# A cross-attention pass of a decoder kernel: folded weights made one pass earlier, zero rows written by SyncE, and another order of the parts

## The reference, cut to what matters

```python
def _L1_xattn_ref(hidden_states, external_embeddings, Wq, bq, Wk, bk, Wv, bv):
    q = hidden_states @ Wq + bq
    k_tok = hidden_states @ Wk + bk
    v_tok = hidden_states @ Wv + bv
    k_ext = external_embeddings @ Wk + bk
    v_ext = external_embeddings @ Wv + bv
    s_self = jnp.einsum('bsh,bsh->bs', q, k_tok)[..., None]
    s_ext = jnp.einsum('bsh,beh->bse', q, k_ext)
    probs = jax.nn.softmax(jnp.concatenate([s_self, s_ext], axis=-1), axis=-1)
    return probs[..., :1] * v_tok + jnp.einsum('bse,beh->bsh', probs[..., 1:], v_ext)

x = x + _L1_attn_ref(_layernorm(x), ...)              # 16 heads of 16
x = x + _L1_xattn_ref(_layernorm(x), ctx_1024, ...)   # the pass that is changed
x = x + _L1_ffn_ref(_layernorm(x), ...)               # top 2 of 8 experts, weighted by their scores
```

## Time and profile before

| | |
|---|---|
| time, three runs | 2931.3, 2927.97, 2929.44 us (median 2929.44) |
| the profiled execution | 2933.47 us, span 2931.6 us |
| mean granted TensorE clock | 0.919 of full |
| TensorE busy | 2398.4 us (82%) |
| VectorE busy | 1984.3 us (68%) |
| ScalarE busy | 1442.5 us (49%) |
| GpSimd busy | 1361.2 us (46%) |
| 16 scatters of zeros twice, L1827 | 973 ns each |

### The profile page before, as it was taken

One profiled execution on the slowest core, in us unless ns is written; L12 is line 12 of the kernel. 1 busy time (PEld: TensorE's weight loads), 2 busy tenths in 40 slices (PEclk: granted clock), 3 DMA queues, 4 the chain that ended last, 5 costly groups with the idle time before them and its releaser, 6 DMA issues. The chain is left out here.

```text
span 2931.6 us, 49210 instructions
## 1 busy us (share of the span) xinstructions
PE 2398.4 (82%) x16164; PEld 1880.4 (64%) x16164; DVE 1984.3 (68%) x4760; ACT 1442.5 (49%) x2778; POOL 1361.2 (46%) x1281
## 2 busy tenths in 40 slices
PE   5888888399999479999999999868888775399880
PEld 3666666389999346566556566547777664399870
DVE  4888888466555268888878888726777665377783
ACT  3666666255555257777777777633333231222220
POOL 5777777454342354444444444114555555000475
PEclk9999999699999789999999999779999897699995
DMA  2222221332220001001001010022222222544795
GB/s 67 62 69 72 59 73 48 75 127 92 61 86 26 29 19 34 26 30 33 26 30 34 26 30 26 19 97 76 90 91 90 91 86 71 164 140 138 222 299 159
DMA packets 205352, 226.68 MB, mean 77 GB/s; under 512 B 32511, under 2 KB 190209, under 8 KB 204849
## 3 DMA queue, kind: packets, MB, share of 16 engines
q1 hardware_dynamic: 181712, 170.85, 18.8%
q0 software_dynamic: 22016, 50.58, 5.5%
q10 hardware_dynamic: 1376, 2.10, 0.2%
HBM read 131.99 MB, written 95.49 MB: 78 GB/s over the span
## 5 line engine op out<-in xcount | busy, mean ns | idle before, releaser
L1320 POOL TENSOR_TENSOR f_hm<-f_hm,f_mhalf 128x64 f32<-128x64 f32 x32 | 347.4, 10855 | 2.7
L1488 DVE TENSOR_REDUCE f_nm<-f_raw 128x4 f32<-128x1024 f32 x256 | 311.9, 1218 | 33.6 <-PE f_raw L1588 33.5
L1381 ACT ACTIVATE f_PT<-f_sco 128x1024 f32<-128x1024 f32 x256 | 262.6, 1026 | 84.6 <-PE f_sco L1606 81.4
L2325 POOL DMA_INDIRECT d_pick<-expert_out,e_out_slots x128 | 131.4, 1027 | 286.2 <-DMA expert_out<-d_eo 233.0
L1588 PE MATMUL f_raw<-f_k4T,f_q4T 64*128 64x256 f32 x1024 | 142.1, 359 | 37.7 <-DVE f_nm L1488 36.9
L895 ACT ACTIVATE b_hT<-b_H,b_b1r 128x512 f32<-128x512 f32 x128 | 88.4, 690 | 163.0 <-PE b_H L1024 147.8
L2344 ACT ACTIVATE d_hh<-d_H 128x512 fp32r<-128x512 f32 x78 | 46.6, 598 | 244.8 <-PE d_H L2438 244.8
L1588 PEld LDWEIGHTS f_raw<-f_k4T,f_q4T 64*128 64x128 f32 x1024 | 85.9, 207 | 106.0 <-DVE f_nm L1488 54.2
L1818 POOL DMA_INDIRECT expert_in<-g_xm,e_slots x128 | 128.6, 1005 | 39.6 <-issue 36.9
L1039 PE MATMUL b_O<-b_w2l,b_hTh 128*128 128x256 f32 x512 | 144.9, 283 | 0.0
L1039 PE MATMUL b_O<-b_w2h,b_hTl 128*128 128x256 f32 x512 | 144.7, 283 | 0.0
(11 more groups left out here) (364 smaller groups left out, 7868.2 us busy)
## 6 DMA issues: line engine op xcount, KB each, us to landing
d_xs<-expert_in SPq DMA_DIRECT2D x78, 256.0 KB, 3.1
expert_out<-d_eo SPq DMA_DIRECT2D x78, 256.0 KB, 2.2
x_scratch<-a_x SPq DMA_DIRECT2D x64, 256.0 KB, 2.7
b_w<-in_L_ffn_W_dram SPq DMA_DIRECT2D x16, 1024.0 KB, 5.7
a_x<-in_x_dram SPq DMA_DIRECT2D x32, 256.0 KB, 3.7
a_cx<-in_ctx_dram SPq DMA_DIRECT2D x32, 256.0 KB, 3.1
f_x<-x_scratch SPq DMA_DIRECT2D x32, 256.0 KB, 2.7
f_xr<-x_scratch SPq DMA_DIRECT2D x32, 256.0 KB, 2.7
```

Source lines behind the costliest of these rows:

```text
L1320: g.tensor_tensor(hm[b % 2][:, :], hm[b % 2][:, :], mhalf[:, :], ALU.pow).then_inc(hroot, 1)
L1381: s.activation(PT[n % 3][:, t, :, :], heads(SCO), ACT.Exp, scale=float(DH) ** -0.5).then_inc(probs_ready, 1)
L1488: v.tensor_reduce(nm[:, t, g * HG:(g + 1) * HG], heads(RAW), AX.X, ALU.max, negate=True)\
L2325: g.indirect_dma_start(pick[b % GR][:, t, c, :], None, ex.eo_d[k], bass.IndirectOffsetOnAxis(ap=ex.out_slots[:, b, t, c:c + 1], axis=0), b ...
```

## The change

Four edits. The fold moves into the first slot of `attention_pass`, behind the v product of batch 0, with banks X and Y for G0 and G1; Wq and Wk become two more weights of `Layer1Weights`, loaded in the phase before. The zero rows at the end of each expert's rows are written by SyncE: per block it reads eight row numbers into a register, each with a DMA of 256 rows. The parts of a slot get another order. Constants and tables that this makes idle go.

```diff
 class Layer1Weights:
+        self.wq_in = [sb("wq_in0", [P, C, D]), sb("wq_in1", [P, C, D])]
+        self.wqk, self.g0, self.wr, self.r0 = sb("wqk", [P, C, D]), sb("g0", [P, C]), sb("wr", [P, C]), sb("r0", [P, 1])
-        self.count = 12
+        self.count = 14
...
+        for tile, name in zip(self.wq_in, ("Wq", "Wk")):
+            weight(tile[:, :, :], by_chunk(a[f"L1_xattn_{name}"]))
...
 attention_pass, scalar, take_v:
+                if b == 0:
+                    fold_cross_weights()
+
+            def fold_cross_weights():
+                act.wait_ge(pro_psum, 1)
+                s.activation(wq_T[0][:, :, :], halves(X), ACT.Copy).then_inc(pro_sb, 1)
+                s.activation(wq_T[1][:, :, :], halves(Y), ACT.Copy).then_inc(pro_sb, 1)
+                act.wait_ge(pro_psum, 2)
+                s.activation(w.wqk[:, :, :], halves(X), ACT.Copy).then_inc(pro_sb, 1)
+                s.activation(w.g0[:, :], Y[:, 0:C], ACT.Copy).then_inc(pro_sb, 1)
...
 attention_pass, tensor, project_v:
+                if b == 0:
+                    fold_cross_weights()
+
+            def fold_cross_weights():
+                transposes(X, w.wq_in[0])
+                transposes(Y, w.wq_in[1]).then_inc(pro_psum, 1)
+                pe.wait_ge(pro_sb, 2)
+                wqT, wkT = wq_T
+                for m in range(C):
...
 cross_pass:
-        ORDER = ("sco gx", "gate norm", "pre stats", "sco scores", "gate T", "file rows", "pre norm", "mix mix", "pre cxT",
-                 "sco exp", "pre T", "mix T", "gate logits", "sco expT", "mix cross", "pre g", "gate ranks")
+        ORDER = (
+            "sco gx", "pre stats", "pre cxT", "gate norm", "sco scores", "gate T", "file rows", "pre norm",
+            "mix mix", "sco exp", "pre T", "sco expT", "mix T", "gate logits", "mix cross", "pre g", "gate ranks")
...
 cross_pass, sync:
-            for tile, name in zip(wq_in, ("Wq", "Wk")):
-                sync.dma_start(tile[:, :, :], by_chunk(a[f"L1_xattn_{name}"])).then_inc(w_in, 16)
...
+            def pad(k):
+                sync.wait_ge(pads_ready, k + 1)
+                for e in range(NE):
+                    row = sync.value_load(pad_row[k][0:1, e:e + 1], min_val=0, max_val=ex.xs_d.shape[0] - ex.TILE)
+                    sync.dma_start(ex.xs_d[bass.ds(row, ex.TILE), :].rearrange("(n p) d -> p n d", p=P),
+                                   zero[:, :].unsqueeze(1).broadcast_to([P, T, D])).then_inc(pads_filed, 16)
+
             for n in range(B + 2):
                 if n + 2 < B:
                     load_x4(n + 2)
                     load_cx(n + 2)
                 if n >= 2:
                     store(n - 2)
+                if n >= 5 and ex.block_of(n - 5)[1]:
+                    pad(ex.block_of(n - 5)[0])
+            pad(NB_ - 1)
...
+            sync.wait_ge(pads_filed, 16 * NE * NB_)
...
 cross_pass, gpsimd, file_rows:
-                k, last = ex.block_of(b)
-                if last:
-                    pool.wait_ge(pads_ready, k + 1)
-                    stand_alone(pool, pool_passed)
-                    for n in range(2):
-                        for e in range(NE):
-                            g.indirect_dma_start(ex.xs_d, bass.IndirectOffsetOnAxis(ap=zidx[k][:, n, e:e + 1], axis=0),
-                                                 zero[:, :], None, bounds_check=ex.xs_d.shape[0] - 1,
-                                                 oob_is_err=False).then_inc(pads_filed, 16)
...
 cross_pass, scalar and tensor: the fold and the waits for pro_sb go (the same instructions as above, with G0 and G1)
 cross_pass, vector:
-            dve.wait_ge(pro_sb, 6)
...
-                v.tensor_tensor(zidx[k][:, :, :], zrow[:, :].unsqueeze(2).broadcast_to([P, 2, NE]),
-                                carried[:, :].unsqueeze(1).broadcast_to([P, 2, NE]), ALU.add).then_inc(pads_ready, 1)
+                v.tensor_scalar(pad_row[k][:, :], carried[:, :], 1.0, None, ALU.add).then_inc(pads_ready, 1)
```

More of the change, by code:

```diff
@@ L1173, in attention_pass @@
         mhalf = sb("mhalf", [P, T * 2 * H])
+        wq_T = sbn("wq_T", 2, [P, C, D])
         selh = sb("selh", [P, H, DH])
@@ L1203, in attention_pass @@
         oT_ready, o_inv = sem("oT_ready"), sem("o_inv")
+        pro_psum, pro_sb = sem("pro_psum"), sem("pro_sb")
         rows = lambda t: t.rearrange("(b t p) d -> b p t d", t=T, p=P)
@@ L1548, in _ @@
             pe.wait_ge(w_centred, 3)
+            pe.wait_ge(w.loaded, 16 * w.count)
             def normT(b):
@@ L1566, in project_v @@
                 project(Z, xnT, wqkv[:, :, 2 * D:3 * D]).then_inc(full("in v"), 1)
+                if b == 0:
[6 more added lines that the diff above has]
+                for m in range(C):
+                    cols = slice(m * P, (m + 1) * P)
+                    for c in range(C):
+                        t_.matmul(halves(X)[:, m, :], wqT[:, c, cols], wkT[:, c, :], start=c == 0, stop=c == C - 1)
+                    for c in range(C):
+                        t_.matmul(Y[:, m:m + 1], wkT[:, c, cols], w.bqT[:, c:c + 1], start=c == 0, stop=c == C - 1)
+                    for c in range(C):
+                        t_.matmul(Y[:, C + m:C + m + 1], wqT[:, c, cols], w.bkT[:, c:c + 1], start=c == 0, stop=c == C - 1)
+                for c in range(C):
+                    last = t_.matmul(Y[:, 2 * C:2 * C + 1], w.bqT[:, c:c + 1].broadcast_to([P, P]), w.bkT[:, c:c + 1],
+                                     start=c == 0, stop=c == C - 1)
+                last.then_inc(pro_psum, 1)
             def splitT(r, b):
@@ L1614, in weigh @@
                 if g == 0:
+                    if b == 0:
+                        pe.wait_ge(pro_sb, 6)
                     wait_taken(pe, "in v", b)
@@ L1668, in cross_pass @@
         iota8 = sb("iota8", [P, NE])
[L1669 to L1672, removed]
+        wvx, bvx, gw, gb = w.wvx, w.bvx, w.gw, w.gb
+        wqk, g0, wr, r0 = w.wqk, w.g0, w.wr, w.r0
         XR, CR, YR = 4, 4, 3
@@ L1729, in slots @@
                         parts[part](b)
-        CONSTS = 14 + NB_
+        CONSTS = 13 + NB_
         block = ctx.enter_context(nc.Block())
@@ L2103, in _ @@
             pe.wait_ge(consts, CONSTS)
[L2104 to L2109, removed]
-                cols = slice(m * P, (m + 1) * P)
-                for c in range(C):
-                    t_.matmul(halves(G0)[:, m, :], wqT[:, c, cols], wkT[:, c, :], start=c == 0, stop=c == C - 1)
-                for c in range(C):
-                    t_.matmul(G1[:, m:m + 1], wkT[:, c, cols], bqT[:, c:c + 1], start=c == 0, stop=c == C - 1)
-                for c in range(C):
-                    t_.matmul(G1[:, C + m:C + m + 1], wqT[:, c, cols], bkT[:, c:c + 1], start=c == 0, stop=c == C - 1)
-            for c in range(C):
-                last = t_.matmul(G1[:, 2 * C:2 * C + 1], bqT[:, c:c + 1].broadcast_to([P, P]), bkT[:, c:c + 1],
-                                 start=c == 0, stop=c == C - 1)
-            last.then_inc(pro_psum, 1)
-            pe.wait_ge(pro_sb, 6)
             def cxT_(b):
```

19 lines of the change are left out of this document (4 added, 15 removed).

## The result

The changed kernel takes 2832.5 us (median of four runs, 2829.3 to 2837.2) where the kernel before takes 2928.7: a ratio of 0.9673, 95% interval 0.9656 to 0.9690. That is 96 us less; forecast were 83, to 2846, in a range of 2828 to 2877. The profiled execution has a span of 2831.9 us for 2931.6.

| stretch | before | after | difference | forecast |
|---|---|---|---|---|
| up to the first v product of the attention pass | 1012.78 | 1013.63 | +0.8 | 0 |
| from there to the first instruction of the cross pass | 929.03 | 924.90 | -4.1 | +1.5 |
| to its first statistics | 15.70 | 2.90 | -12.8 | -12 |
| to the last bias copy (g_gT) | 481.43 | 416.46 | -65.0 | -58.1 |
| to the first instruction of the experts' phase | 67.89 | 46.87 | -21.0 | -15.2 |

A forecast was written before the change was run, and what follows sets the result against it. TensorE has the largest share, but a cross-engine chain sets the 14.15 us cross-pass slot. Terms -12 + 1.5 - 33 - 8 - 17.1 - 15.2 = -83.8 give 2849.7 profiled, 2846 us as median; range 2828 to 2877.

The forecast's parts named there:

- Head: Start of the cross pass: with the fold gone, VectorE's first statistics come earlier, -12 us (bounds -10 and -12.2).
- Fold into the attention pass: Behind the first v product: TensorE's next instruction moves 6.5 us, 4.45 covered by a wait; +1.5 us (bounds 0, +6).
- Order of parts: Steady cross-pass slot: 14.15 us falls to 13.0, in 29 intervals, -33 us (bounds -12 and -54).
- rival E: Cross pass: slots at TensorE's own 12.3 us and no long ones, 2822 us; chance 0.07.
- Long slots: Seven cross-pass slots, 1.65 us longer at the lower clock, lose waits: -8 us (bounds 0 and -11.6).
- First block of zero rows: Mid-pipeline: without GpSimd's 16 scatters the interval of 31.23 us becomes 14.15, -17.1 us (bounds -15, -17.1).
- Second block: Tail before the next phase: SyncE's zero rows land at 2486.3 instead of 2501.5, -15.2 us (bounds -11.7, -20.5).
- A: Cross-pass slot: order gives little, a new chain on ScalarE or VectorE, long slots stay; 2875 us, chance 0.17.
- B: Cross-pass slot: moved norm of y holds up GpSimd's second sum 0.40 us per slot; 2858 us, chance 0.12.
- The prediction's sign of being wrong, TensorE waiting for gxs: Cross pass: the forecast is wrong if TensorE waits for GpSimd's gxs; no size given.
- C: Cross pass: granted clock falls in every slot, 29 x 1.65 = 48 us; 2902 us, chance 0.05.
- D: Zero rows: SyncE's reads and DMAs take t each, slower kernel from t = 7.5 us; 2937 at t = 8, chance 0.02.

The follow-up runs named there:

- filler: The kernel before, with TensorE making the transposes of xn twice in each slot; 2918.1 us, 0.9966.
- pads_only: The kernel before, with the zero rows written by SyncE and nothing else changed; 2891.2 us, 0.9868.
- split_pads: The changed kernel with VectorE's table steps spread over nine slots and ScalarE issuing four of the last eight zero blocks; 2823.7 us, 0.9635.
- norm_first: The changed kernel with VectorE's norm of y and of the gates put back ahead of its statistics of the next x; 2843.4 us, 0.9706.
- expT_back: The changed kernel with transposes and copy of the exponentials put back behind the gate logits, just ahead of the cross products; 2835.8 us, 0.9690.

## Why the prediction was right, step by step

**Head, -12 forecast, -12.8 measured.** Right. The x4 load was not the limit; VectorE waits for GpSimd's constants, 2.9 us into the pass instead of the 3.5 assumed for the load. The load was near: issued at 1938.53, with the shortest landing of that stretch, 2.7 us, it is there at 1941.2, and the statistics start at 1941.43.

**Fold into the attention pass, +1.5.** The mechanism is shown: the next instruction moved by 6.2 (6.5 forecast), 4.45 of it lay in a wait for VectorE, and a second fold, which moved it by another 10.97, cost 7.9. The net size is known only as 0 to 5 us: by run times 2.8, by the means of the traces 0.4. The forecast lies inside.

**Order of parts, -33.** 29 x 1.23 = -35.7. The working gave 12.92 and the slot takes 12.92. No two errors met there by luck: its four steps came out within 0.07 us each (3.32, 4.76, 6.76, 8.23 for 3.33, 4.76, 6.83, 8.22). The 0.08 that were added "for hops from engine to engine" were not there. Hops were already in the rows that were summed. TensorE's own work, 12.92 - 0.61 = 12.31, agrees with the 12.28 of rival E, and does not bind yet.

**Long slots, -8.** All seven went: -11.8. The mechanism (fewer waits in the low part) agrees with filler; the step was sized between "some" and "all" without a row that says which.

**First block of zero rows, -17.1.** Right: 31.23 us against 14.14 in pads_only.

**Second block, -15.2.** Mis-sized: -21.0. Eight blocks took SyncE 8.94 us instead of 10.2. Above all, between the last issue and the next phase lie 3.38 us; the prediction had put 3.1 for the landing and had kept another 5.3, the time that passes in the earlier trace rows between a scatter's median landing and the next phase. That rest belongs to GpSimd's scatters and not to the change of phase: SyncE's writes need 3.38 in all. SyncE started 0.7 later than assumed. 1.3 + 5.0 - 0.7 = 5.6 of the 5.8 us. So the term that was mis-sized is the time from the end of SyncE's issues to the next phase: 8.4 in the working, 3.38 measured. The result lies by the bound of -20.5, where the last filed rows bind; as split_pads shows, they would bind 0.38 us earlier.

**Together.** 0.8 + 2.7 + 3.8 + 5.8 = 13.1 us more gain than forecast in the cross pass; the median lies 13.5 under the forecast time. The other differences between the two traces, -5.6 ahead of the statistics that the fold does not explain and +2.4 in the unchanged experts' phase, are no larger than what single executions differ by (the attention pass by 8 us, the experts' phase 423.1 to 429.1 us over the fourteen traces), and the profiled pair shows 3.5 us more than the medians.

**Rivals.** A is out: the exp copy and the gates made no new chain. B is out, as norm_first shows with the norm even earlier than in the change: GpSimd's sum still starts 0.05 us ahead of it and keeps its 1.26 us, and it is VectorE that takes 2.16. The prediction's sign of being wrong, TensorE waiting for gxs, came once in 31 slots (0.20 us), and GpSimd's sums had their usual length there. The rule of the Trainium skill (SBUF — State Buffer, "Who interferes with whom") that the first comer keeps the lock agrees with those rows; no row here shows this norm come first. That GpSimd can be the one held up is seen in the attention pass of before, where a step of 0.25 us takes 1.11 when it starts 0.27 us behind two sums of VectorE:

```profile
1013.69 0.25 POOL L1318 TENSOR_SCALAR f_hm<-f_hm 128x64 f32<-128x64 f32 x1 [7.40 <-DVE f_hm L1452]
...
1028.23 1.28 DVE L1466 TENSOR_TENSOR f_qk<-f_qk,c_gam 128x512 f32<-128x512 f32 x2
1028.50 1.11 POOL L1318 TENSOR_SCALAR f_hm<-f_hm 128x64 f32<-128x64 f32 x1 [2.09 <-DVE f_hm L1452]
```

C is out, the clock went up. D is out at 1.12 us a block. E: the long slots went as it says, the slot did not reach TensorE's own work.

## What to carry to other kernels

Walk one steady slot's chain across engines row by row and take the sum as it stands: the hops are in the rows. Short waits of TensorE cost twice here, once as waits and again when the clock fell for the products behind them (1.69 us in each of seven slots), so a slot with several of them is worth reordering, or filling with useless work, even where they are off the chain. A part that moves ahead of another can depend on a third move (expT on cxT); time the moves singly before believing in any. Work that only the next phase needs goes into the waits of many slots, not into one.

## What the runs showed of the hardware that was not expected

- 0.45 us of useless transposes in each slot of 14.15 us made the kernel 12.3 us faster: the granted clock of 20 slots rose from 0.97 to 1.00, although no wait in a slot had been above 0.87 us. Waits of TensorE in a slot, in us, and long slots in 31: 0.61 none, 0.96 none (norm_first), 1.05 none (expT_back), 1.43 none (filler), 1.87 five to seven (four traces), 2.55 fifteen.
- Between the end of GpSimd's last scatter and the next phase lie 7.0 to 7.7 us in every trace. Where SyncE's last write of 256 KB comes late enough to count, the next phase follows the end of its issue by 3.37 to 3.41 (nine traces).
- One stretch of unchanged code, the attention pass, differs by 8 us between single executions (920.9 to 929.0 in five traces), which is more than several of the terms under test. In steps of 5 us its granted clock shows 20 to 24 stretches below 0.95, and they fall at other times in each trace.
